# Maxima over partitions by transposition and a product with ones, and the last batch's side work spread over its steps

## The reference

```
xn = layernorm(x)
s  = attention(xn)           # 16 heads of 32, causal, ALiBi bias, softmax, output projection
g  = silu(moe(xn))           # 2 experts, top-1 routing, weight = the router's softmax value
out = x + s * g

moe: h = xn @ w_fc[e].T      # 512 -> 2048
     a = where(h >= 0, h, 0.5 h) ** 2
     y = a @ w_proj[e].T     # 2048 -> 512
```

## Time and profile before

| | |
|---|---|
| median of 3 executions | 1516.79 us (1515.6 to 1517.38) |
| profiled execution | 1518.39 us |
| its span, first to last instruction | 1516.3 us |
| TensorE busy | 1400.7 us, 92% |
| VectorE busy | 927.6 us, 61% |
| ScalarE busy | 770.7 us, 51% |
| GpSimd busy | 686.0 us, 45% |

### The profile page before, as it was taken

How to read it: one execution, slowest core, us unless ns; L and a number is a source line. 1 busy time by engine, 2 the same in 40 slices (tenths; PEclk the granted TensorE clock), 3 DMA queues, 4 the chain that set the end, 5 groups by cost and what they waited for, 6 DMA issues and landing times.

```text
span 1516.3 us, 30035 instructions
## 1 busy us (share of the span) xinstructions
PE 1400.7 (92%) x9860; PEld 886.5 (58%) x9860; DVE 927.6 (61%) x2438; ACT 770.7 (51%) x1824; POOL 686.0 (45%) x897
## 2 busy tenths in 40 slices
PE   2879999999999999999569999999999999999995
PEld 1445555655556565555336666666666666666663
DVE  7477677777766777776638954544455554444443
ACT  3377777786877778687626532222222222222221
POOL 0365657465665746565514433333333333233332
PEclk9999999999999999999879999999999999999998
DMA  4424324342533434244217511001111110101100
GB/s 157 140 84 146 121 92 154 109 135 84 160 106 94 153 109 135 85 140 136 91 65 242 180 43 38 27 26 39 43 42 41 38 43 29 29 29 43 35 29 29
DMA packets 84897, 133.45 MB, mean 88 GB/s; under 512 B 14095, under 2 KB 63247, under 8 KB 82576
## 3 DMA queue, kind: packets, MB, share of 16 engines
q1 hardware_dynamic: 75808, 105.70, 22.2%
q0 software_dynamic: 8944, 25.83, 5.5%
HBM read 97.81 MB, written 33.95 MB: 87 GB/s over the span
## 4 chain that ended last, share of the span: by engine, by line
PE 72%; DVE 12%; POOL 7%; issue 5%; ACT 3%; DMA 1%; DVEq 1%; SPq 0%; POOLq 0%; ACTq 0%
PE psF L1090 19%; PE psY L1110 19%; PE psA L348 18%; PE psT L442 7%; PE psA L457 5%; POOL pr L920 4%; PE psS L421 2%; DVE sg L1287 2%; PE psX L1064 1%; POOL route L953 1%; DVE pr L837 1%; ACT stage L507 1%; DVE stat L729 1%; PE psA L405 1%; DVE wf L1209 1%
## 5 line engine op out<-in xcount | busy, mean ns | idle before, releaser
L1090 PE MATMUL psF<-xT,wf 128*128 128x256 f16 (+1 forms) x3264 | 368.0, 269 | 0.0
L1110 PE MATMUL psY<-wf,aT 128*128 x1584 | 363.9, 379 | 0.4 <-DVE aT L1254 0.4
L1090 PEld LDWEIGHTS psF<-xT,wf 128*128 x3264 | 312.0, 98 | 63.6
L920 POOL TENSOR_SCALAR pr<-pr,rden 128x128 f32<-128x128 f32 (+3 forms) x512 | 269.7, 547 | 146.5 <-DVE rden L848 138.0
L1328 POOL TENSOR_TENSOR a<-a 128x512 f32<-128x512 f32 (+1 forms) x136 | 152.5, 1122 | 392.8 <-DVE a L1245 391.4
L567 ACT ACTIVATE pr<-pr,mn 128x128 f32<-128x128 f32 (+3 forms) x512 | 281.9, 553 | 0.0
L837 DVE CUSTOM_DVE_ANT_0 pr<-psS,base,nsl 128x128 f32<-128x128 f32 (+3 forms) x512 | 249.8, 543 | 2.4 <-PE psS L421 2.0
L1110 PEld LDWEIGHTS psY<-wf,aT 128*128 128x128 f16 x1584 | 154.5, 98 | 158.6 <-issue 1.1
L442 PE MATMUL psT<-conf,pr 128*128 128x128 f32 x1280 | 210.1, 283 | 34.4 <-POOL pr L920 30.5
L442 PEld LDWEIGHTS psT<-conf,pr 128*128 128x128 f32 x1280 | 160.5, 145 | 100.8 <-POOL pr L920 39.3
L1167 ACT ACTIVATE rl<-psF 128x512 f32<-128x512 f32 (+1 forms) x136 | 79.4, 584 | 265.3 <-PE psF L1090 265.1
(11 more groups left out here) (149 smaller groups left out, 1378.0 us busy)
## 6 DMA issues: line engine op xcount, KB each, us to landing
qk_parts<-pre SPq DMA_DIRECT2D x64, 256.0 KB, 2.3
qs<-qk_parts SPq DMA_DIRECT2D x128, 128.0 KB, 2.7
ks<-qk_parts SPq DMA_DIRECT2D x128, 128.0 KB, 2.7
wst<-in_wf SPq DMA_DIRECT2D x16, 1024.0 KB
wstage<-in_wf SPq DMA_DIRECT2D x32, 512.0 KB, 4.7
xin<-in_x SPq DMA_DIRECT2D x32, 256.0 KB
attn_out<-so SPq DMA_DIRECT2D x32, 256.0 KB, 2.0
pt<-in_wqkv SPq DMA_DIRECT2D x4, 768.0 KB, 9.9
```

The lines of the kernel that those rows point to most:

```text
L920: nc.gpsimd.tensor_scalar(p_, p_, rden[:, c:c + 1], 32768.0, ALU.mult, ALU.mult).then_inc(s["norm_done"], 1)
L1090: last = nc.tensor.matmul(psF[c % 2][:, k * TT:k * TT + tn], w(e, 2 * hc, hl, kc * 512 + col, P), xT[:, r % 2, x, kc, 0:tn], start=(m == 0 ...
L1110: last = nc.tensor.matmul(psY[r % 2][h][:], aT[:, c % 4, x, k, h * P:(h + 1) * P], w(e, 2 * hc + 1, hl, q * 512, 512), start=(c == 0 and k ...
```

## The change

`weight_scales` no longer takes its maxima from GpSimd. After step 12 TensorE transposes `fam` to two rows of 128; in step 13 VectorE takes the maximum of each row, bounds it and multiplies it into a 2x2 diagonal (`weight_row`); after step 13 TensorE multiplies a 2x128 matrix of ones with this diagonal, which puts both maxima on all partitions; in step 14 `weight_scales` reads them from PSUM. Both TensorE instructions use the bank psA0.

`route()` is cut in four parts for steps 1, 3, 5 and 6. The fetches of tiles 0 and 1 go to steps 8 and 10. The two gathers of tile 0 go to steps 10 and 12; the gathers of tile 1 go to the step before last of the expert stage's lead-in, behind the first squaring. Pieces 0 and 1 are split in step 15, pieces 2 and 3 in step 0 of the extra iteration; in step 15 VectorE's norm comes first, as it did ahead of pieces 2 and 3.

```diff
+ROUTE_AT = (1, 3, 5, 6)
+        famd = sb("famd", [2, 2], F32)
+        ones2 = sb("ones2", [2, P], F32)
...
     (TensorE, att_tensor)
+                if b == B - 1 and step == 12:
+                    pe.wait_ge(s["wm_link"], 4 * B)
+                    pe.wait_ge(s["O_evac"], (B - 1) * QB)
+                    nc.tensor.transpose(psA[0][0:2, 0:P], fam[:, 0:2], conf[:, C_ID:C_ID + P]).then_inc(s["fam_turned"], 1)
+                if b == B - 1 and step == 13:
+                    pe.wait_ge(s["fam_row"], 1)
+                    nc.tensor.matmul(psA[0][:, 0:2], ones2[:], famd[:], start=True, stop=True
+                                     ).then_inc(s["fam_spread"], 1)
                 if b == B - 1 and step >= 14:
                     ffn["xtrans"](pe, 0, step - 14)
     (ScalarE, att_scalar)
-                if b == B - 1 and step >= 14:
-                    ffn["split_hi"](act, range(2 * step - 28, 2 * step - 26))
+                if (b, step) in ((B - 1, 15), (B, 0)):
+                    ffn["split_hi"](act, range(2 * (step == 0), 2 * (step == 0) + 2))
     (VectorE, att_vector: route(part) runs instructions 1-4, 5-8, 9-12, 13-17)
+        def weight_row():
+
+            dve.wait_ge(s["fam_turned"], 1)
+            setup(nc.vector.tensor_reduce(fam[0:2, 3:4], psA[0][0:2, 0:P], AX.X, ALU.max))
+            setup(ts(fam[0:2, 3:4], fam[0:2, 3:4], 1e-9, None, ALU.max))
+            ts(famd[:], conf[0:2, C_ID:C_ID + 2], fam[0:2, 3:4], None, ALU.mult).then_inc(s["fam_row"], 1)
...
         def weight_scales():
 
-            dve.wait_ge(s["allmax"], 2)
-
-            setup(ts(x(X_PA1, 2), x(X_PA1, 2), 1e-9, None, ALU.max))
-            setup(ts(x(X_PA1, 2).bitcast(I32), x(X_PA1, 2).bitcast(I32), 0x7F800000, None, ALU.bitwise_and))
+            dve.wait_ge(s["fam_spread"], 1)
+            setup(ts(x(X_PA1, 2).bitcast(I32), psA[0][:, 0:2].bitcast(I32), 0x7F800000, None, ALU.bitwise_and))
...
-                if b == B - 1 and step == 6:
-                    route()
-                if b == B - 1 and step == 9:
+                if b == B - 1 and step in ROUTE_AT:
+                    route(ROUTE_AT.index(step))
+                if b == B - 1 and step in (8, 10):
                     dve.wait_ge(s["m_in"], 16)
-                    ffn["fetch"](dve, 0, 0)
-                    ffn["fetch"](dve, 1, 1)
+                    ffn["fetch"](dve, step // 2 - 4, step // 2 - 4)
                 if b == B - 1 and step == 13:
-                    weight_scales()
+                    weight_row()
                     ffn["norm"](dve, 0, 0, 0)
                 if b == B - 1 and step == 14:
-                    ffn["split_lo"](dve, range(0, 2))
+                    weight_scales()
                 if b == B - 1 and step == 15:
                     ffn["norm"](dve, 0, 1, 0)
+                    ffn["split_lo"](dve, range(0, 2))
+                if b == B and step == 0:
                     ffn["split_lo"](dve, range(2, 4))
     (GpSimd, att_gpsimd)
-                if b == B - 1 and step == 10:
-                    ffn["gather_x"](pool, 0, 0)
-                    ffn["gather_x"](pool, 1, 1)
-                if b == B - 1 and step == 12:
-                    pool.wait_ge(s["wm_link"], 4 * B)
-                    nc.gpsimd.partition_all_reduce(sc[:, X_PA1:X_PA1 + 2], fam[:, 0:2], P, RMAX
-                                                   ).then_inc(s["allmax"], 1)
+                if b == B - 1 and step in (10, 12):
+                    ffn["gather_x"](pool, 0, 0, (step // 2 - 5,))
     (GpSimd, ffn_gpsimd)
-                if c == 0 and 0 <= n < SLOTS - 2:
-                    gather_x(pool, n + 2, r + 2)
+                if c == (0 if n >= 0 else GR - 2) and within(n + 2, 1, SLOTS):
+                    gather_x(pool, n + 2, r + 2, range(halves(n + 2)))
```

More of the change, by code:

```diff
@@ L208, in attention_block @@
              "R_done R_part R2_done logits_read rank_read e_ready nd_ready rexp_done meta_ready m_in wmax_in wmax_done "
-             "apart_dve apart_sp apart_pool dve_link wm_link pool_link meta_out routed scaled").split()
+             "apart_dve apart_sp apart_pool dve_link wm_link pool_link meta_out routed scaled "
+             "fam_turned fam_row fam_spread").split()
     s = {n: sem(n) for n in names}
@@ L604, in att_vector @@
         nc.vector.memset(fam[:], 0.0)
+        nc.vector.memset(ones2[:], 1.0)
         nc.vector.memset(ones16[:], 1.0)
@@ L676, in prepare, with route @@
             dve.wait_ge(s["bout_in"], 16)
-        def route():
+        def route(part):
             LAST = SLOTS - 1
[L681 to L700, removed]
@@ new lines, in route @@
+            if part == 0:
+                setup(ts(n0[:, 0:1], esum[:, 0:1], -1.0, float(TOK), ALU.mult, ALU.add))
+                setup(ts(n0[:, 0:1], n0[:, 0:1], float(TOK - 1), None, ALU.min))
+                setup(nc.vector.tensor_copy(n0i[:, 0:1], n0[:, 0:1]))
+                setup(ts(n0i[:, 1:2], n0i[:, 0:1], P, None, ALU.bitwise_and))
+            if part == 1:
+                setup(ts(n0i[:, 0:1], n0i[:, 0:1], TOK - P, None, ALU.bitwise_and))
+                setup(nc.vector.tensor_copy(n0[:, 1:3], n0i[:]))
+                setup(ts(eslot[:], conf[:, C_SLOT:C_SLOT + SLOTS], n0[:, 0:1], None, ALU.is_gt))
+                setup(ts(eslot[:, LAST:SLOTS], n0[:, 2:3], 1.0 / P, None, ALU.mult))
@@ new lines, in route @@
+            if part == 2:
+                setup(ts(n0[:, 3:4], n0[:, 1:2], -1.0, float(TOK - P), ALU.mult, ALU.add))
+                setup(ts(tf[:], eslot[:], n0[:, 2:3], -1.0, ALU.mult, ALU.mult))
+                setup(nc.vector.tensor_tensor(tf[:], tf[:], conf[:, C_SLOT:C_SLOT + SLOTS], ALU.add))
+                setup(ts(tint[:], tf[:], 1.0 / P, -1.0, ALU.mult, ALU.add))
+            if part == 3:
+                setup(ts(tf[:, 0:1], eslot[:, LAST:SLOTS], n0[:, 3:4], n0[:, 1:2], ALU.mult, ALU.add))
+                setup(ts(tint[:, LAST:SLOTS], tf[:, 0:1], 1.0 / P, None, ALU.mult))
+                setup(ts(eint[:], eslot[:], eslot[:, 0:1], None, ALU.not_equal))
+                setup(ts(ebase[:, 0:1], eslot[:, 0:1], 2.0 * HC, None, ALU.mult))
+                ts(ebase[:, 1:2], eslot[:, 0:1], -2.0 * HC, 2.0 * HC, ALU.mult, ALU.add).then_inc(s["routed"], 1)
+                dve.wait_ge(s["routed"], 1)
@@ L1304, in ffn_vector, with gather @@
         slots(dve, step)
-    def gather(dst, src, n, r, sm):
-        for h in range(halves(n)):
+    def gather(dst, src, n, r, sm, which):
+        for h in which:
             nc.gpsimd.indirect_dma_start(
@@ L1311, in gather, with gather_x @@
                 in_offset=bass.IndirectOffsetOnAxis(ap=gidx[:, r % 4, h:h + 1], axis=0)).then_inc(sm, 16)
-    def gather_x(pool, n, r):
-        if n == 0:
+    def gather_x(pool, n, r, which):
+        if n == 0 and which[0] == 0:
             pool.wait_ge(att["xT_done"], QB * B)
         wait(pool, s["idx_ready"], n + 1, s["apart_pool"])
-        gather(xg[:, r % 4, :, :], io["x"], n, r, x_got[r % 4])
+        gather(xg[:, r % 4, :, :], io["x"], n, r, x_got[r % 4], which)
     def ffn_gpsimd(pool):
@@ L1341, in step @@
                             pool.wait_ge(s_out[i], 16 * (B + 1))
-                    gather(sg[:, r % 2, :, :], io["s"], n, r, s_got[r % 2])
+                    gather(sg[:, r % 2, :, :], io["s"], n, r, s_got[r % 2], range(halves(n)))
         slots(pool, step)
```

## The result

| | before | after |
|---|---|---|
| median | 1516.84 us (4 runs) | 1497.19 us (1495.18 to 1500.34, 4 runs) |
| profiled execution, its span | 1518.39, 1516.3 | 1497.08, 1495.3 |
| TensorE busy | 1400.7 (92%) | 1392.0 (93%) |
| mean granted clock | 0.975 | 0.984 |

Ratio 0.9874, 95% interval 0.9855 to 0.9892: 19.1 us less, 16.4 to 22.0.

A forecast was written before the change was run, and what follows sets the result against it. A chain of waits in the last attention batch was taken as the bound. Output products 15.75 us sooner, less 0.5 in the expert stage, gave 15.2, taken as 15.0: 1501.8 us from 1516.8; range 1497.5 to 1508.

The forecast's parts named there:

- What bounds it, and the all-reduce: Last attention batch: a chain of waits bounds it; removing the all-reduce takes both gaps, 13.2 us, from GpSimd.
- only the all-reduce pays: Rival: before head 12 other ring members replace each removed wait; 9.7 less 0.5 us gained, 1507.6 us; chance 0.2.
- Routing: Steps 1, 3, 5, 6: spreading the 17 instructions starts head 8 sooner, 2.2 us; parts in 1, 3, 5 mostly hidden.
- Fetches and gathers up to head 12: Steps 8 to 12: with routing, head 12's transposes start at 738.3 instead of 745.71, 7.4 us gained.
- Head 12 to head 15: End of last batch: head 12 starts at 738.3, head 15 at 751.5; TensorE's wait for the row costs 1.3 us.
- the clock stays up: Rival: the denser ring keeps 2.4 GHz for heads 12 to 14, context and output products; 18.4 us, 1498.4; chance 0.12.
- The row's own price: Steps 12 to 14: transposition and product 0.15 to 0.3 us each, three small VectorE instructions 0.6, maximum 0.2 to 0.75.
- Gathers of tile 1: Expert stage: landing 2.5 us after issue, up to twice that; loss 0 to 1.3 us, taken as 0.5.
- a sign of a wrong step: Among those listed: VectorE waiting for a gather at either normalization; over 14 us from head 15 to the output products.
- The tail: From head 15 to first output product: 12.8 us against 12.58, 0.2 worse, read-out behind weight piece 4 and its DMA.
- The output products: After the tail: they start at 764.3 instead of 780.05, 15.75 us sooner, with no further loss before the expert stage.
- the ring: Last batch: path of transposes, exponentials, reciprocal, normalization across four engines; head 15 at 751.5 against 767.47, 16.0 us sooner.

The follow-up runs named there:

- e3: Kernel before with an ordinary GpSimd multiplication by 1 of the same two columns in place of the all-reduce; 1506.9 us, ratio 0.9938.
- e1: Kernel before with only the all-reduce replaced (transposition, row maximum, product; weight pieces moved); routing, fetches and gathers as they were; 1505.5 us, ratio 0.9922.
- e2: Changed kernel with the all-reduce kept in step 12 behind the gather and weight pieces where they were before; 1511.2 us, ratio 0.9972 to the kernel before.
- e5: Changed kernel with all 17 routing instructions in step 6 again; 1500.8 us, ratio 0.9903 to the kernel before.
- e7: Changed kernel with all four gathers back in step 10; 1503.1 us, ratio 0.9919 to the kernel before.
- e6: Changed kernel with both fetches back in step 9; 1499.9 us, ratio 0.9908 to the kernel before.
- e9: Changed kernel executed again, unaltered, beside later runs; 1499.0 us, ratio 0.9885 to the kernel before.
- e8: Changed kernel with the last context read out and cast ahead of weight pieces 2 to 5 and their low halves; 1493.7 us, ratio 0.9863 to the kernel before.
- e4: Kernel before with the all-reduce executed twice in a row, the first into unused columns; 1517.2 us, ratio 1.0004.
- e11: e10 with eight discarded 512-column products on TensorE ahead of the output products; 1492.7 us, ratio 0.9842 to the kernel before.
- e10: e8 with the last context's products ahead of the transposes of the tile's second half on TensorE; 1492.8 us, ratio 0.9847 to the kernel before.

## Why the prediction was right, and where its sizes were off

- **What bounds it, and the all-reduce.** Right. Both gaps left with it (e3), and the price of the reduction alone is 9.4 us in e1's profile, for which the rival "only the all-reduce pays" had 9.7. It was not the only one: e2 gains too.
- **Routing.** 2.2 us forecast, 2.2 found, in the change and undone in e5. The parts in steps 1, 3 and 5 have no visible cost.
- **Fetches and gathers up to head 12.** 7.4 forecast, 7.54 found. The parts of it: gathers 3.8 (e7), routing 2.2, fetches 1.3 (e6).
- **Head 12 to head 15: the term that was mis-sized.** The walk had 13.2 us (its own terms, 748.2 + 2.39 + 1.12, give 13.4), measured 11.3. It ran heads 12 and 13 and the context at half clock (2.39 and 3.4 us), where even before only head 12 and the context had; they ran at full clock (1.31 and 2.36), and head 13 came 4.9 us after head 12 instead of 6.1, held by GpSimd. TensorE did stand 1.33 us for VectorE's row, as priced, but it costs nothing: the product ran at 741.86, and head 14 then still waited 0.27 for GpSimd. This is the rival "the clock stays up", half come true: for heads 12 and 13 and not for the output products. In e9 heads 14 and 15 took 2.39 and 2.40 us and head 15 came no later (30.8), so only the first two and the context count. Added by that: 1.9 us.
- **The row's own price.** Transposition 0.27 us, maximum over 128 elements 0.27, two instructions 0.14 and 0.42, product 0.38: inside the bounds, but for the 0.42, twice the 0.2 of a small instruction.
- **Gathers of tile 1.** VectorE did wait for both landings, 0.94 and 1.14 us, which I had listed as a sign of a wrong step. It cost nothing: the reciprocal of head 15 came at 743.20, 0.04 after the exponentials that it needs, and the tile's transposes came 13.07 us after the first expert product in both kernels. The landing took 4.6 us beside the weight stream (issued by 779.5, in use at 784.19), near the double of 2.5 that I allowed. The 0.5 us of loss was not there.
- **The tail.** 12.8 us forecast to the output products, 13.47 measured (745.59 to 759.06). That the read-out stands behind piece 4 and its DMA is right: e8 turns that order round, and they start 11.4 us after head 15. In e9 the tail was 14.06, just over the 14 that I had named as a sign of a wrong step; head 15 took 2.40 us there and 1.87 in the first profile. No run has the new places of the weight pieces alone. The low half of piece 0 took 1.88 us for 1.1, beside ScalarE's work.
- **The output products, a term put at nothing.** The walk let the first expert product come 12.0 us after them, as before. It came 12.7 after (13.1 in e9), behind a wait of 7.35 us where there had been 2.68: 0.7 lost (1.1), at a clock of 0.81 over 760 to 770.
- **Sum.** Against the 15.2 us that the terms add up to, the ring gave 2.0 more and the gathers 0.5 more, the tail and the output products 0.7 less each: 16.4. So the total is nearer than its terms, which is partly luck. Forecast 15.0; 16.4 from head 7 on in the first profile, 15.5 in the second, and 19.1 and 17.4 by the medians. Between the two profiles the rest is mostly clock ahead of the changed steps, which no profile of before could have given; that the same makes up the rest of the medians' 19.1 is likely, not shown. The range was cut too close on that side: I had priced the clock for the changed steps alone, while head 7's start by itself scatters over 6.8 us.

## What to carry to other kernels

The one all-reduce of 0.37 us cost GpSimd 6.01 us ahead of it and 7.19 behind it. For an instruction of a rare kind look for "issue" on both sides and for the ordinary work that waits behind; the same reduction in a stretch where GpSimd waited anyway cost nothing ahead of it. When a ring of four engines is the path, walk it with durations at both clocks: here heads 12 and 13 ran at the full one once the waits were gone. Compare the parts of a change at a point ahead of anything that the clock can shorten, or they seem to add up by chance. And anchor two profiles at the last instruction that no edit touches before adding up where the time went.

## What the runs showed of the hardware that I had not expected

- Way in and way back of an all-reduce are paid once each for a pair in a row: 5.85 and 6.83 us around two (e4), 6.01 and 7.19 around one. Each is opened by two MODIFY_POOL_CONFIG records, at 749.0 and 755.1 in the kernel before.
- The same wait of 1.8 us on TensorE was or was not followed by a fall to 1.2 GHz; each fall cost about 1.7 us, and with their number moved the start of head 7 between 714.1 and 720.8 us in thirteen profiles.
- With eight discarded products in what was a wait of 4.28 us the clock was 1.00, and the 48 products behind them took 1.3 us less (e11, one execution against one of e10).
